# Attention over 128 graphs: transposes and small-tile matmuls regrouped in TensorE's queue, the bias factor folded into a reduction, a QK copy and a scaling placed elsewhere

## The reference

```python
q, k, v = split_heads(x @ Wq.T), split_heads(x @ Wk.T), split_heads(x @ Wv.T)
bias = (adj + adj)[:, None]
a = jnp.einsum('bhnd,bhmd->bhnm', q, k) * D ** -0.5 + bias
row_nonzero = jnp.any(a != 0, axis=-1, keepdims=True)   # rows that are all zero give p = 0
p = softmax(where(row_nonzero, a, -inf)); p = where(isnan(p), 0, p)
o = jnp.einsum('bhnm,bhmd->bhnd', p, v)
x1 = layernorm(x + merge_heads(o) @ Wo.T)
```

## Time and profile before

| what | value |
|---|---|
| median of 3 runs | 2996.41 us (2993.43 to 2997.7) |
| the profiled execution's own time | 2996.29 us |
| its span | 2994.5 us |
| TensorE busy | 2844.9 us (95%) |
| VectorE busy | 2244.9 us (75%) |
| ScalarE busy | 1477.0 us (49%) |
| GpSimd busy | 1306.5 us (44%) |
| granted TensorE clock, mean | 0.979 |
| DMA | 277.30 MB, mean 93 GB/s |

### The profile page before, as it was taken

The page is one execution under the profiler, slowest core; times in us unless marked ns, Lnnn a source line. Parts: engine busy times, 40 slices in busy tenths (PEclk is TensorE's granted clock), DMA queues, the critical chain, the costliest instruction groups (busy, mean ns, idle before and its releaser), DMA issues. The chain is left out here.

```text
span 2994.5 us, 79322 instructions
## 1 busy us (share of the span) xinstructions
PE 2844.9 (95%) x22786; PEld 2247.5 (75%) x22787; DVE 2244.9 (75%) x8929; ACT 1477.0 (49%) x5261; POOL 1306.5 (44%) x1171
## 2 busy tenths in 40 slices
PE   8999999999999999999999999999699999997776
PEld 7888888888888888888888888888477777775322
DVE  6777777777777777777777777777677777775998
ACT  5555555555555555555555555555422222221444
POOL 2343334333333333343333333333256666665786
PEclk9999999999999999999999999999699999997898
DMA  3111111111111111111111111111133433334998
GB/s 140 54 53 47 59 49 50 49 57 49 50 49 57 53 46 60 49 50 49 57 49 50 49 57 51 48 55 44 65 122 123 128 124 125 127 120 165 376 373 327
DMA packets 169425, 277.30 MB, mean 93 GB/s; under 512 B 19378, under 2 KB 52146, under 8 KB 168882
## 3 DMA queue, kind: packets, MB, share of 16 engines
q1 hardware_dynamic: 150962, 243.36, 24.8%
q10 hardware_dynamic: 18432, 33.56, 2.9%
HBM read 184.57 MB, written 92.27 MB: 92 GB/s over the span
## 5 line engine op out<-in xcount | busy, mean ns | idle before, releaser
L529 POOL TENSOR_TENSOR probs<-probs,row_scale 128x512 f32<-128x512 f32 x512 | 562.9, 1099 | 1293.7 <-DVE row_scale L418 1281.0
L324 ACT ACTIVATE probs<-neg_s,neg_max 128x128 f32<-128x128 f32 x2048 | 792.6, 389 | 81.9 <-DVE neg_max L394 81.9
L394 DVE CUSTOM_DVE_ANT_0 neg_s<-att_bank,neg_bias 128x128 f32<-128x128 f32 x2048 | 443.0, 287 | 139.1 <-PE att_bank L201 139.1
L324 ACT ACTIVATION_READ_ACCUMULATOR probs<-neg_s,neg_max 128x1 f32 x2048 | 384.9, 188 | 0.0
L352 ACT ACTIVATE probs_t<-att_bank 128x512 f32<-128x512 f32 x256 | 153.0, 598 | 459.8 <-PE att_bank L239 459.8
L403 DVE TENSOR_REDUCE abs_max<-neg_s 128x4 f32<-128x512 f32 x512 | 340.5, 665 | 0.0
L178 PE MATMUL att_bank<-xt_hi,att_w_hi 128*128 128x256 f32 x2048 | 329.2, 283 | 11.0 <-DVE att_w_lo L373 11.0
L178 PE MATMUL att_bank<-xt_lo,att_w_hi 128*128 128x256 f32 x2048 | 329.7, 283 | 0.0
L178 PE MATMUL att_bank<-xt_hi,att_w_lo 128*128 128x256 f32 x2048 | 329.7, 283 | 0.0
L460 DVE TENSOR_TENSOR o_lo<-att_bank,o_hi 128x512 fp32r<-128x512 f32 x128 | 88.5, 691 | 318.5 <-ACT o_hi L355 318.5
L178 PEld LDWEIGHTS att_bank<-xt_hi,att_w_hi 128*128 128x128 f32 x2048 | 290.9, 192 | 20.4 <-issue 10.6
(11 more groups left out here) (121 smaller groups left out, 5506.9 us busy)
## 6 DMA issues: line engine op xcount, KB each, us to landing
xt_stage<-in_x_t SPq DMA_DIRECT2D x64, 512.0 KB, 3.5
x_nat<-in_x SPq DMA_DIRECT2D x128, 256.0 KB, 2.6
x_scratch<-x SPq DMA_DIRECT2D x128, 256.0 KB, 2.0
g_x<-x_scratch SPq DMA_DIRECT2D x128, 256.0 KB, 2.8
n_x<-x_scratch SPq DMA_DIRECT2D x128, 256.0 KB, 5.6
out_x<-n_out ACTq DMA_DIRECT2D x128, 256.0 KB, 5.7
y_scratch<-g_out SPq DMA_DIRECT2D x96, 256.0 KB, 2.0
n_y<-y_scratch SPq DMA_DIRECT2D x96, 256.0 KB, 5.1
```

Source lines behind the costliest of these rows:

```text
L324: nc.scalar.activation(probs[:, h * P:(h + 1) * P], neg_s[:, h * P:(h + 1) * P], ACT.Exp, bias=neg_max[:, h:h + 1], scale=-1.0, accum_out= ...
L394: nc.vector.tensor_tensor_reduce(neg_s[:, h * P:(h + 1) * P], bank[r][:, c * P:(c + 1) * P], neg_bias[:, s % 2], 1.0, BIG, ALU.add, ALU.mi ...
L529: nc.gpsimd.tensor_tensor(part, part, by, ALU.mult).then_inc(probs_done, 1)
```

## The change

The values products are no longer spread among the transposes and the small-tile products: all 16 transposes come first, then six values products, then the 32 records of `weighted_values`, the scores in one piece, and the other six values products. QK unit 0 moves from behind the output projection to ahead of it. On ScalarE three exponentials move ahead of the copy of the values, and the second QK copy comes after the last exponential. On VectorE -2 adj is not computed any more: Q is scaled by half of D ** -0.5, and the reduction multiplies the sum by -2. The first quarter's maximum, inverse and scale and the second quarter's maximum move ahead of `res`; the high part of x moves behind the second copy; the QK copy of unit 1 stays behind the statistics. On GpSimd the normalisation of the third quarter moves ahead of the power.

```diff
-    SCALE = float(D) ** -0.5
+    HALF_SCALE = 0.5 * float(D) ** -0.5
 SyncE:
-                    sp.wait_ge(bias_done, t + 1)
+                    sp.wait_ge(min_done, HEADS * (t + 1))
 TensorE:
-                some_values(2)
                 transposes(0)
                 transposes(1)
-                some_values(4)
                 transposes(2)
-                some_values(1)
-                weighted_values(0)
                 transposes(3)
-                some_values(1)
-                weighted_values(1)
-                some_values(1)
-                weighted_values(2)
-                weighted_values(3)
+                some_values(6)
+                for c in range(C):
+                    weighted_values(c)
                 if exists(t, last, 1):
                     for done in qk_done:
                         pe.wait_ge(done, 2 * (t + 1 - (s + 1) % 2) + 4)
-                    pe.wait_ge(pt_even, 2 * t + 2)
-                    pe.wait_ge(pt_odd, 2 * t + 2)
-                    scores((s + 1) % UNROLL, lambda: some_values(3))
+                    scores((s + 1) % UNROLL)
+                some_values(6)
+                def next_unit(k):
+                    ahead = s + 3
+                    if k == 0 and s % 2:
+                        pe.wait_ge(xt_lo_done, i * 2 + ahead // 2 + 1)
+                    pe.wait_ge(qk_done[k % 2], AHEAD // 2 + 2 * t + k // 2)
+                    qk_unit(AHEAD + 4 * t + k, k, ahead % 2, (ahead // 2) % 2, BANK_B - k % 2)
+                more_units = exists(t, last, 3)
+                if more_units:
+                    next_unit(0)
 (output projection)
+                if more_units:
+                    for k in range(1, UNITS):
+                        next_unit(k)
 ScalarE:
+                if exists(t, last, 1):
+                    exps(t + 1, range(0, 3))
                 if exists(t, last, 2):
                     copy_v(t + 2, (s + 2) % UNROLL, BANK_WO)
-                for k, heads in ((0, range(0, 8)), (2, range(8, 14)), (None, range(14, HEADS))):
+                for k, heads in ((0, range(3, 9)), (2, range(9, HEADS))):
 VectorE:
-                                                   bank[r][:, c * P:(c + 1) * P], neg_bias[:, s % 2],
-                                                   1.0, BIG, ALU.add, ALU.min,
+                                                   bank[r][:, c * P:(c + 1) * P], adj_nat[:, s],
+                                                   -2.0, BIG, ALU.add, ALU.min,
                 if more:
                     dve.wait_ge(s_ps, t + 2)
-                    dve.wait_ge(bias_done, t + 2)
-                    minima(t + 1, s + 1)
+                    minima(t + 1, (s + 1) % UNROLL)
+                    largest(t + 1, 0)
+                    inverse(t + 1, 0)
+                    scales(t + 1, 0)
+                    largest(t + 1, 1)
 (res)
                 if more:
-                    largest(t + 1, 0)
-                    inverse(t + 1, 0)
+                    inverse(t + 1, 1)
+                    scales(t + 1, 1)
 (bn_stats)
-                if more:
-                    scales(t + 1, 0)
-                dve.wait_ge(stats_done, t + 1)
                 if exists(t, last, 3):
                     copy_qk(AHEAD + 4 * t + 1, 1, ahead % 2, (ahead // 2) % 2)
+                dve.wait_ge(stats_done, t + 1)
+                if more:
+                    largest(t + 1, 2)
+                    inverse(t + 1, 2)
+                    scales(t + 1, 2)
 (bn_aggr)
-                if more:
-                    inverse(t + 1, 1)
-                    largest(t + 1, 1)
-                    scales(t + 1, 1)
-                    inverse(t + 1, 2)
-                    largest(t + 1, 2)
 GpSimd:
                     normalise(t + 1, 1)
+                    normalise(t + 1, 2)
                 pool.wait_ge(ve_done, t + 1)
 (power)
                 if exists(t, last, 1):
-                    normalise(t + 1, 2)
                     normalise(t + 1, 3)
```

More of the change, by code:

```diff
@@ L66, in attention_phase @@
         adj_nat = sb("adj_nat", [P, UNROLL, P])
-        neg_bias = sb("neg_bias", [P, 2, P])
         qk = sb("qk", [P, 2, 2, C, GN])
@@ L98, in attention_phase @@
         xt_hi_done, xt_lo_done = sem("xt_hi_done"), sem("xt_lo_done")
-        bias_done = sem("bias_done")
         qk_ps = sem("qk_ps")
@@ L191, in v_parts, with scores @@
                     yield
-            def scores(s, halfway=lambda: None):
+            def scores(s):
                 par, j = (s // 2) % 2, s % 2
                 for c in range(C):
-                    if c == C // 2:
-                        halfway()
                     for r in range(HC):
@@ L318, in copy_qk @@
                 nc.scalar.activation(qk[:, par, which, c, :], bank[BANK_B][:, 0:GN], ACT.Copy,
-                                     scale=-SCALE if which == Q else 1.0).then_inc(qk_done[0], 1)
+                                     scale=HALF_SCALE if which == Q else 1.0).then_inc(qk_done[0], 1)
             def exps(t, heads):
@@ L356, in body @@
                                      ACT.Copy).then_inc(o_hi_done, 1)
+                ahead = s + 3
+                if exists(t, last, 1):
+                    exps(t + 1, range(0, 3))
                 if exists(t, last, 2):
                     copy_v(t + 2, (s + 2) % UNROLL, BANK_WO)
-                ahead = s + 3
-                for k, heads in ((0, range(0, 8)), (2, range(8, 14)), (None, range(14, HEADS))):
+                for k, heads in ((0, range(3, 9)), (2, range(9, HEADS))):
                     if exists(t, last, 1):
                         exps(t + 1, heads)
-                    if exists(t, last, 3) and k is not None:
+                    if exists(t, last, 3):
                         copy_qk(AHEAD + 4 * t + k, k, ahead % 2, (ahead // 2) % 2)
@@ L382, in copy_qk, with minima @@
                 nc.vector.tensor_scalar(qk[:, par, which, c, :], bank[BANK_A][:, 0:GN],
-                                        -SCALE if which == Q else 1.0, None, ALU.mult).then_inc(qk_done[1], 1)
-            def bias(t, s):
+                                        HALF_SCALE if which == Q else 1.0, None, ALU.mult).then_inc(qk_done[1], 1)
+            def minima(t, s):
                 dve.wait_ge(adj_in[s], (t - s) * 4 + 16)
-                nc.vector.tensor_scalar(neg_bias[:, s % 2], adj_nat[:, s], -2.0, None,
-                                        ALU.mult).then_inc(bias_done, 1)
-            def minima(t, s):
+                dve.sem_inc(minima_begun, 1)
                 for h in range(HEADS):
@@ L425, in _ @@
             cut_w(K)
-            bias(0, 0)
             cut_xt(1, 1)
@@ L433, in _ @@
             dve.wait_ge(s_ps, 1)
-            dve.wait_ge(bias_done, 1)
             minima(0, 0)
@@ L451, in body @@
                         copy_qk(AHEAD + 4 * t - 1, C - 1, s % 2, ((s + 2) // 2) % 2)
[L452 to L457, removed]
-                        nc.vector.tensor_copy(xt_hi[:, s // 2], xt_stage[:, s // 2]).then_inc(xt_hi_done, 1)
+                if s % 2 and not last:
+                    dve.wait_ge(v_ps, t + 1)
+                    dve.wait_ge(xt_in[s // 2], i * 16 + 32)
+                    nc.vector.tensor_copy(xt_hi[:, s // 2], xt_stage[:, s // 2]).then_inc(xt_hi_done, 1)
                 dve.wait_ge(o_hi_done, t + 1)
@@ L464, in body @@
                     dve.wait_ge(s_ps, t + 2)
-                    dve.wait_ge(bias_done, t + 2)
-                    dve.sem_inc(minima_begun, 1)
-                    minima(t + 1, s + 1)
+                    minima(t + 1, (s + 1) % UNROLL)
[3 more added lines that the diff above has]
+                    largest(t + 1, 1)
                 dve.wait_ge(wo_ps, t + 1)
@@ L496, in body @@
                 if more:
-                    scales(t + 1, 2)
                     largest(t + 1, 3)
```

## The result

The changed kernel takes 2862.8 us (median of 4 runs, 2861.5 to 2862.95) against 2996.11 of the kernel before in the same comparison: ratio 0.9557, 95% interval 0.9541 to 0.9572. That is 133 us less; the forecast was 124 (2872 us). Its profiled execution has a span of 2860.9 us and a mean granted clock of 0.98.

What follows compares the result with a forecast made beforehand. TensorE's own queue was taken to bound the 16.49 us step; 1.17 us saved at borders less a 0.18 stall gives 15.50, 0.99 over 125 steps is 124 us off 2996.3: 2872 us, 8-in-10 range 2846 to 2924.

Steps and rivals of the forecast that it cites:

- The borders: TensorE changes between full-array and 32-wide tiles: fewer of them save 1.17 us a step, TensorE's own step becoming 15.32 us.
- The stall of the last transposes: TensorE waits for GpSimd's fourth normalisation: 0.13 us plus 0.05 for restarting the queue, 0.18 a step.
- The two ends of the phase: Last three attention steps wait for GpSimd anyway: 0, give or take 3 us; expert and norm phases untouched.
- The moved QK unit: QK unit 0 between values and projection covers ScalarE's copy of the values: cost 0, at most 0.5 us if late.
- The fold of -2: Takes one 128x128 operation per step off VectorE: worth 0 to 0.1 us, taken as 0.
- the wait of `res`: New VectorE idle time before res, waiting for the projection: about 0.7 us, from 5.2 to 5.87 after the scores.
- x1 held behind the fourth normalisation: Shared VectorE/GpSimd port: normalisation goes first and x1 waits, nothing added; other order adds 0.24 to 0.34, step 15.8 us.
- the sixteen transposes in a row: TensorE's 16 transposes, no values product between: 1.73 us; copies hidden behind six values products, cost 0, else up to 0.5.
- No stall: Rival: last transposes do not wait; 1.17 us saved in each of 125 steps, 146 us, 2850 us; chance 0.18.
- A longer stall: Rival: fourth normalisation 0.4 to 0.9 us late, saving 0.3 to 0.8 a step, 2896 to 2960 us; chance 0.22.
- the borders were waits in disguise: Rival: border costs are later instructions' waits and come back, about 2996 us; gaining nothing has chance 0.05.
- The clock: Rival: TensorE's clock falls to the 1.2 GHz level in the transposes and small-tile stretch, about 3375 us; chance 0.05.

Runs made afterwards that it cites:

- a_t3_later: Changed kernel with two of the six values products moved ahead of the last four transposes; 2845.22 us, ratio 0.9500.
- b_products: Kernel before with the four probability products in one piece, values products and last transposes between them moved ahead, scores as before; 2917.27 us, ratio 0.9738.
- a_border: Changed kernel with one values product put between the second and third probability product, five ahead instead of six; 2903.85 us, ratio 0.9697.
- the two score experiments: b_scores, and the kernel before with scores in one piece, their three values products ahead of the last two probability products: 3004.04 us.
- a_unit0_back: Changed kernel with QK unit 0 put back behind the output projection; 2993.53 us, ratio 0.9994 to the kernel before.
- b_scores: Kernel before with the scores in one piece and their three values products behind them, all else as before; 3051.36 us, ratio 1.0188.
- a_power_first: Changed kernel with GpSimd's power put back ahead of the third normalisation; 2945.05 us, ratio 0.9832 to the kernel before.
- b_pe_new: Kernel before with the changed kernel's whole TensorE queue; ScalarE, VectorE, GpSimd and bias as before; 3172.92 us, ratio 1.0593.
- b_others_new: Kernel before with the new VectorE and GpSimd queues and the folded -2; TensorE and ScalarE as before; 2999.79 us, ratio 1.0016.

## Why the prediction was right

*The borders.* Worked out 1.17 us a step, to 15.32; a_t3_later runs at 15.33. The rows at the borders were the right place to read: "busy 16.46 of 16.49" had no idle time to take out, and 6% of the step went all the same (7% in a_t3_later). b_products, a_border and the two score experiments each give the price of their borders within 0.03 us a step, once the waits seen in the trace are taken off.

*The stall of the last transposes.* This is the term that was mis-sized: 0.18 forecast, 0.10 found in three steps of four and 0.19 in the fourth, 0.13 in the mean. The chain's instants came true to 0.03 us up to the last scale; the fourth normalisation ended 0.07 earlier than worked out, and the last transposes came 0.04 late where 0.13 was forecast. The restart behind the wait, taken as 0.05, is 0.06. In one step of four `res` starts 0.29 us after TensorE has begun the products behind the projection, and not 0.20, and the whole chain comes 0.1 later; the cause of that is open. The mean stall gives 0.05 x 125 = 6 us of the 9 between 124 and 133.

*The two ends of the phase.* The rest lies outside the full steps. In the profiled executions the first 125 distances between projections save 129.6 us (1.04 each), and the last two 1.9, where the prediction had 0, give or take 3. The first projection starts 0.9 us later (46.1 before, 47.0 after). Behind the start of the last projection (2137.0 and 2006.4) the changed kernel needs 3.0 us less, a term that the prediction did not have; 1.9 of it is that projection itself, which ran at a granted clock of 0.50 before and of 1.00 after. Together that is 133.6, the difference of the spans.

*The moved QK unit.* Cost 0, cover for the copy of the values: right, and the warning was sized too small. The prediction said that a late copy would cost at most 0.5; without the cover it costs 0.98 (a_unit0_back), which is more than nine tenths of the gain of the whole change. The same oversight made the expectation of b_scores wrong.

*The fold of -2* at nothing, the wait of `res` (0.6 idle where 0.7 was forecast), x1 held behind the fourth normalisation, and the sixteen transposes in a row at no cost of their own: as forecast. a_power_first shows the other order of x1 and the normalisation at its price: 0.65 us a step together with the later start. The Trainium skill's rule on the shared port ("SBUF — State Buffer", "Who interferes with whom") fits: 0.53 and 2.42 in one order, 1.25 and 1.04 in the other.

*The rivals.* No stall: forecast as 2850 us, and a_t3_later, which has none, takes 2845. A longer stall, 2.2 us a step over TensorE's own 15.33, is what happens when only TensorE's queue changes (b_pe_new). That the borders were waits in disguise is excluded by b_others_new and b_products together. The clock: in the changed kernel it stayed at 1.00 from 14.9 to 1984.4 us of the span, with sixteen transposes in a row in every step, so the rule of the Trainium skill in "TensorE: Matmul & The Clock Gate", "Part 4: PE-mode transpose", that transposes do not count as TensorE activity in the same way, had no effect that this trace can show. The clock does fall in mid phase in b_pe_new, which has the same sixteen transposes, but broken by two waits for GpSimd. So a fall of the clock does cost this kernel time (1.62 us in each step that has one), but sixteen transposes in a row do not bring it about by themselves.

## What to carry to other kernels

An engine that is busy all the time can still be wasting time: measure from start to start at the places where the kind of instruction changes, take off what the same instructions cost in the middle of a row of their kind, and multiply. Before instructions are gathered into one block, list for each one what ran in its shadow (here the copy of the values and the low part of the output), because taking the interruption out takes the cover away too. And when two arrangements have the same number of borders, choose the one that leaves the other engines the most time: a chain that misses by 0.04 us costs 0.10.

## What was not expected of the hardware

A transpose group whose data is late by 0.04 us delays TensorE by 0.10: 0.149 and 0.165 us between starts that are 0.109 apart otherwise, as the 0.10 in 3.32 against 3.22 shows.

The price of an uncovered copy of 0.60 us is 0.86 to 1.04. In b_scores the copy starts 0.21 after the values products have had their time (1010.81 against 1010.60), and the projection 0.05 after its end; in a_unit0_back the copy first waits for the third exponential, 0.35 (1003.50 against 1003.15). The start-up of the projection behind the pause, 0.10, comes on top.

The granted clock can fall in the middle of a phase in which TensorE is busy for 16.05 of 17.50 us: in b_pe_new it did so once in four steps, for 3.4 us, behind waits of 0.85 and 0.72 us. a_power_first, with one wait of 0.54 us a step, stayed at 1.00 in mid phase.
